# A recommendation net: the last part's second half worked off by feature groups, its layer 0 without transposes back, and the logits as 16 rows

## The reference, cut to what matters

```python
x = dense_inputs                                   # 2048 x 13
for W, b, g, be in bot:                            # 13 -> 512 -> 256 -> 64
    x = _bn(relu(x @ W + b), g, be)                # batch norm over all 2048 rows
embs = vmap(lambda tbl, idx: tbl[idx])(emb_tables, sparse_inputs)   # 26 rows of 64 for each batch
T = concatenate([embs, x[:, None, :]], axis=1)     # 27 vectors of 64
Z = einsum('bnd,bmd->bnm', T, T)                   # all pairs
R = concatenate([x, Z[:, iu, ju]], axis=1)         # 64 + 351 columns
h = R
for W, b, g, be in top:                            # 415 -> 512 -> 256 -> 1
    h = _bn(relu(h @ W + b), g, be)
return sigmoid(h)
```

## Time and profile before

| what | value |
|---|---|
| median of three runs | 573.51 us (572.97 to 573.55) |
| profiled execution, its own time | 573.65 us |
| its span, first to last instruction | 571.8 us |
| TensorE busy, weight loads busy | 374.6 us (66%), 281.1 us (49%) |
| VectorE, ScalarE, GpSimd busy | 238.8 us (42%), 189.5 us (33%), 388.8 us (68%) |
| mean granted clock of TensorE | 0.763 of full speed |
| chain that ended last, by engine | POOL 55%, issue 19%, PE 18% |

### The profile page before, as it was taken

How to read it: one execution, slowest core, us unless ns; L and a number is a source line. 1 busy time by engine, 2 the same in 40 slices (tenths; PEclk the granted TensorE clock), 3 DMA queues, 4 the chain that set the end, 5 groups by cost and what they waited for, 6 DMA issues and landing times.

```text
span 571.8 us, 16640 instructions
## 1 busy us (share of the span) xinstructions
PE 374.6 (66%) x5806; PEld 281.1 (49%) x5827; DVE 238.8 (42%) x650; ACT 189.5 (33%) x509; POOL 388.8 (68%) x419
## 2 busy tenths in 40 slices
PE   5959768678687572755729181754738182777995
PEld 2328536566565462543517171553526172566682
DVE  5773354644445342424323242423324242455522
ACT  4752144434244141323214041322314041464223
POOL 5777777777777777777777777777777777770100
PEclk9999886896786877585857666585858567598999
DMA  8322122222212221222122121222212121220000
GB/s 240 62 29 28 28 27 31 30 26 31 30 29 30 27 31 29 31 27 30 27 28 30 28 31 26 30 27 29 31 29 29 26 30 26 30 28 7 2 0 2
DMA packets 17500, 18.49 MB, mean 32 GB/s; under 512 B 9302, under 2 KB 10589, under 8 KB 17278
## 3 DMA queue, kind: packets, MB, share of 16 engines
q0 software_dynamic: 13088, 13.43, 17.6%
q1 hardware_dynamic: 4330, 3.96, 2.3%
HBM read 17.35 MB, written 0.01 MB: 30 GB/s over the span
## 4 chain that ended last, share of the span: by engine, by line
POOL 55%; issue 19%; PE 18%; DVE 2%; ACT 2%; DMA 1%; SPq 0%; POOLq 0%; DVEq 0%; ACTq 0%
POOL emb L367 52%; PE l_bank L442 6%; PE l_bank L458 5%; POOL emb L380 3%; PE l_bank L448 3%; PE l_bank L472 2%; PE l_bank L564 1%; DMA emb<-table,stage 1%; ACT Zs L306 1%; PE z_bank L400 1%; DMA par<-params 1%; DVE TT L916 0%; PE l_bank L611 0%; PE l_bank L561 0%; PE tr_bank L536 0%
## 5 line engine op out<-in xcount | busy, mean ns | idle before, releaser
L367 POOL DMA_INDIRECT emb<-table,stage x385 | 363.9, 945 | 120.3 <-issue 117.1
L306 ACT ACTIVATE Zs<-z_bank 27x112 f32<-27x112 f32 (+3 forms) x272 | 92.1, 339 | 200.8 <-PE z_bank L507 179.5
L493 PE MATMUL tr_bank<-ident,emb 128*128 128x128 f32 x195 | 39.1, 330 | 125.8 <-DMA emb<-table,stage 105.5
L280 DVE COPY Zs<-z_bank 27x112 f32<-27x112 f32 (+3 forms) x272 | 88.6, 326 | 51.1 <-PE z_bank L507 43.6
L521 PE MATMUL l_bank<-Zs,tw_sb 128*128 128x128 f32 x840 | 107.2, 281 | 0.0
L521 PEld LDWEIGHTS l_bank<-Zs,tw_sb 128*128 128x128 f32 x840 | 103.1, 199 | 0.0
L916 DVE COPY TT<-tr_bank 128x512 f32<-128x512 f32 (+1 forms) x60 | 54.6, 975 | 97.3 <-PE tr_bank L493 96.8
L493 PEld LDWEIGHTS tr_bank<-ident,emb 128*128 128x128 f32 x195 | 25.9, 163 | 137.5 <-issue 104.0
L507 PE MATMUL z_bank<-TT 64*27 64x26 f32 x3840 | 63.5, 219 | 31.8 <-issue 18.4
L507 PEld LDWEIGHTS z_bank<-TT 64*27 64x27 f32 x3840 | 55.4, 134 | 42.1 <-issue 38.1
L927 DVE BATCH_NORM_STATS2 stats_t<-h_part 128x128 f32 x60 | 17.7, 294 | 112.7 <-ACT hidden_hi L705 110.1
(11 more groups left out here) (130 smaller groups left out, 279.2 us busy)
## 6 DMA issues: line engine op xcount, KB each, us to landing
emb<-table SPq DMA_DIRECT2D x640, 0.2 KB
emb<-table,stage POOLq DMA_INDIRECT x409, 2.8
emb_sp<-table SPq DMA_DIRECT2D x256, 0.2 KB
tw_sb<-tw0x SPq DMA_DIRECT2D x1, 1792.0 KB
bw_sb<-bw SPq DMA_DIRECT2D x1, 512.0 KB, 3.8
tw_sb<-tw SPq DMA_DIRECT2D x1, 512.0 KB
twx_sb<-twx SPq DMA_DIRECT2D x1, 256.0 KB
idx_raw<-idx SPq DMA_DIRECT2D x1, 169.0 KB, 2.5
```

What stands on the lines that cost most here:

```text
L280: last = copy(dst, src[:, :, ZC * q:ZC * q + w])
L306: return nc.scalar.activation(dst, src, ACT.Copy)
L367: pool.indirect_dma_start(out=emb[:, s, k, h, :], out_offset=None, in_=table, in_offset=bass.IndirectOffsetOnAxis(ap=stage[:, s, col:col + ...
L493: tr = nc.tensor.transpose(tr_bank[g % 2][:, c * P:(c + 1) * P], emb[:, s, k, :, :].rearrange("p h d -> p (h d)"), ident[:, :])
```

## The change

Five things change.

1. The second half of the last part gets groups of its own, pairs 0 to 6, 6 to 12 and 12 to 13 (the first keeps its three groups). x becomes feature 0 of TT, the embeddings 1 to 26, and a pair's tile column c and quadrant q are now the quotient and rest of the second feature by four; so columns c 0 to 2 of Zs need only the first group, 3 to 5 the second, 6 the third. Z, its copies and layer 0 follow group by group.
2. In that half a Z matmul takes a block of batches: two in the first two groups, four in the third. The half has its own tile TT_last with 32 columns for a batch, so the stationary operand is 64 or 128 columns, and the moving one the group's features of all batches of the block (2 x 12, 2 x 12, 4 x 2). Only the blocks of a batch with itself are copied (take_last: eight copies per engine of 13x48, eight of 25x48, four of 27x16). The first half's Z goes to one bank and is copied in 8 copies per engine; all copies from Z now read every fourth column.
3. Layer 0 of the last part has the weights stationary, as in the loop, 128 batches at once, column by column c, each for all four blocks, started when its c is there. pre0, last_back and the four transposes back are gone. Relu is four ScalarE operations of 128x128; the high parts of the last part are made behind w1_hi, and layer 1 waits for last_lo only before its fourth chunk. The number of idle matmuls in the last part changes from 7, 2, 1, 5, 15 to 7, 2, 10, 8, 1, 7, 11.
4. The logits are written as 16 rows of 128 batches: for each of the two k 16 matmuls of 32 columns over 128 batches, whose weight has one column that isn't zero, in place of 4 over 512. ScalarE's three operations are 128x128, mean_of picks the 16 rows by a column of par, and 16 rows of 512 bytes are stored in place of 4 of 2 KB.
5. At the start VectorE computes the row numbers for SyncE before it clears Zs, and clears TT_last and tw2_col too.

```diff
-LAST_GROUPS = ((0, 8), (8, 12), (12, 13))
+Z_BATCHES = (2, 2, 4)
+LAST_GROUPS = (((0, 8), (8, 12), (12, 13)), ((0, 6), (6, 12), (12, 13)))
...
+        def take_last(copy, g, quadrants):
+            c0, c1 = group_tiles(*LAST_GROUPS[1][g])
+            m0, m1 = NQ * c0, min(NQ * c1, NF)
+            rows = m1 + 1
+            for j in quadrants:
+                z = Z_BATCHES[g]
+                src = last_z_bank[1][g][QUAD * j:QUAD * j + rows, 0:RX * z * (m1 - m0)].rearrange(
+                    "p (x b m) -> p x b m", b=z, m=m1 - m0)[:, :, j % z, :]
+                for q in range(NQ):
+                    m = quadrant_columns(q, c0, c1)
+                    if not len(m):
+                        continue
+                    dst = Zs[QUAD * q:QUAD * q + rows, c0:c0 + len(m), :].rearrange(
+                        "p c (h x j) -> p h x j c", h=2, j=NQ)[:, 1, :, j, :]
+                    last = copy(dst, src[:, :, m[0] - m0:m[-1] + 1 - m0:NQ])
+            return last
...
-                if net == "top":
-                    pe.wait_ge(last_lo, K0)
                 for ch in range(CHUNKS):
+                    if net == "top" and ch == CHUNKS - 1:
+                        pe.wait_ge(last_lo, K0)
...
+            def last_z_group(g):
+                first = len(LAST_GROUPS[0])
+                pe.wait_ge(last_tt_v, first + g + 1)
+                if g < len(LAST_GROUPS[1]) - 1:
+                    pe.wait_ge(last_tt_a, first - 1 + g + 1)
+                c0, c1 = group_tiles(*LAST_GROUPS[1][g])
+                m0, m1 = NQ * c0, min(NQ * c1, NF)
+                z = Z_BATCHES[g]
+                w = z * (m1 - m0)
+                for x in range(RX):
+                    for j in range(0, NQ, z):
+                        some = last_T(1)[:, x * NQ + j:x * NQ + j + z, :]
+                        mm = nc.tensor.matmul(last_z_bank[1][g][QUAD * j:QUAD * (j + z), x * w:(x + 1) * w],
+                                              some.rearrange("p b n -> p (b n)"), some[:, :, m0 + 1:m1 + 1],
+                                              start=True, stop=True)
+                mm.then_inc(last_z_done, 1)
+
+            def last_layer0(c, blocks=range(K0)):
+                part = slice(LAST * 2 * UNIT, B)
+                for o in blocks:
+                    cols = slice(o * P, (o + 1) * P)
+                    if c < 0:
+                        mm = nc.tensor.matmul(l0_bank[o][:, 0:2 * UNIT], twx_sb[:, cols], x_all[:, part],
+                                              start=True, stop=False)
+                    else:
+                        mm = nc.tensor.matmul(l0_bank[o][:, 0:2 * UNIT], tw0_sb[:, c, cols], Zs[:, c, :],
+                                              start=False, stop=(c == ZC - 1))
+                    if c == ZC - 1:
+                        mm.then_inc(last_l0, 1)
...
             keep_clock(7, z_bank[0])
+            last_z_first()
+            pe.wait_ge(l0_relu, LAST * K0)
+            last_layer0(-1)
+            keep_clock(2, tr_bank[1])
             last_transposes(1, 0)
+            keep_clock(10, tr_bank[1])
+            last_z_group(0)
+            keep_clock(8, tr_bank[1])
+            last_taken(1)
+            last_taken(2)
+            last_layer0(0)
+            last_layer0(1)
             last_transposes(1, 1)
+            last_layer0(2)
+            keep_clock(1, tr_bank[0])
+            last_z_group(1)
             last_transposes(1, 2)
+            keep_clock(7, tr_bank[1])
+            last_taken(3)
+            last_layer0(3)
+            last_z_group(2)
+            last_layer0(4)
+            last_layer0(5)
+            last_taken(4)
+            last_layer0(6, (0, 2, 1, 3))
+
+            keep_clock(11, z_bank[0])
             layer1("top")
...
-                for j in range(CHUNKS):
-                    mm = nc.tensor.matmul(out_bank[0][QUAD * j:QUAD * (j + 1), :], tw2_rep[:, k, :],
-                                          hidden1[:, k, j * CHUNK:(j + 1) * CHUNK],
-                                          start=(k == 0), stop=(k == K1 - 1))
+                for j in range(LB):
+                    for q in range(NQ):
+                        first = (q * LB + j) * P
+                        mm = nc.tensor.matmul(out_bank[0][QUAD * q:QUAD * (q + 1), 0:P],
+                                              tw2_col[:, k, j * QUAD:(j + 1) * QUAD], hidden1[:, k, first:first + P],
+                                              start=(k == 0 and j == 0), stop=(k == K1 - 1 and j == LB - 1))
```

More of the change, by code:

```diff
@@ L70 @@
 CHUNKS = B // CHUNK
-CU = CHUNK // UNIT
+LB = CHUNK // P
+LROW = QUAD // LB
 PW = NF
@@ L96, with quadrant_columns, group_tiles @@
 PARAMS["top", "W", 2] = (sum(w for _, w in PARAMS.values()), K1)
-NPARAM = sum(w for _, w in PARAMS.values())
+NPARAM = sum(w for _, w in PARAMS.values()) + 1
 def group_pairs(g):
     return range(g * GROUP, min((g + 1) * GROUP, TP))
-def quadrant_columns(q):
-    return min(ZC, NF - ZC * q)
+def quadrant_columns(q, c0=0, c1=ZC):
+    return range(q + NQ * c0, min(q + NQ * c1, NF), NQ)
+def group_tiles(k0, k1):
+    return k0 // 2, (k1 + 1) // 2
 def rec_program(nc, idx, sp_idx, table, dense_t, params, identity, bw0, bw1, bw2, tw0x, twx, tw1, out):
@@ L539, in last_transposes @@
                 tr.then_inc(last_transposed, 1)
-            def last_z(h):
-                pe.wait_ge(last_tt_v, (h + 1) * len(LAST_GROUPS))
-                pe.wait_ge(last_tt_a, upper_copies((h + 1) * len(LAST_GROUPS)))
-                pe.wait_ge(tt_x_written, PARTS)
-                for y in range(2):
-                    for x in range(y * RX // 2, (y + 1) * RX // 2):
-                        for j in range(NQ):
-                            one = TT[0:D, h, x * NQ + j, :]
-                            mm = nc.tensor.matmul(z_bank[y][QUAD * j:QUAD * j + V, x * ZM:(x + 1) * ZM],
-                                                  one, one[:, 1:V], start=True, stop=True)
-                    mm.then_inc(last_z_done, 1)
@@ L554, in last_layer0 @@
-            def last_layer0(h, t, columns):
-                for c in columns:
-                    for f in range(2):
-                        acc = l0_bank[t][f * UNIT:(f + 1) * UNIT, 0:P]
-                        cols = slice(f * HALF + t * P, f * HALF + (t + 1) * P)
-                        if c < 0:
-                            mm = nc.tensor.matmul(acc, x_all[:, last_columns(h)], twx_sb[:, cols],
-                                                  start=True, stop=False)
-                        else:
-                            mm = nc.tensor.matmul(acc, Zs[:, c, h * UNIT:(h + 1) * UNIT],
-                                                  tw0_sb[:, c, cols], start=False, stop=(c == ZC - 1))
-                return mm
@@ L586, in _, with last_z_first @@
-            for g in range(len(LAST_GROUPS)):
+            def last_z_first():
+                for x in range(RX):
+                    for j in range(NQ):
+                        one = last_T(0)[:, x * NQ + j, :]
+                        mm = nc.tensor.matmul(last_z_bank[0][QUAD * j:QUAD * j + V, x * ZM:(x + 1) * ZM],
+                                              one, one[:, 1:V], start=True, stop=True)
+                mm.then_inc(last_z_done, 1)
[8 more added lines that the diff above has]
+                w = z * (m1 - m0)
+                for x in range(RX):
+                    for j in range(0, NQ, z):
[3 more added lines that the diff above has]
+                                              start=True, stop=True)
+                mm.then_inc(last_z_done, 1)
@@ L1050 @@
     for row, (n, m) in enumerate(zip(*np.triu_indices(V, k=1))):
-        q, c = divmod(m - 1, ZC)
-        tw0x[QUAD * q + n, c] = w0[D + row]
+        first, second = (0, n) if m == NF else (n + 1, m)
+        c, q = divmod(second, NQ)
+        tw0x[QUAD * q + first, c] = w0[D + row]
     cols = idx.reshape(UNIT * 2, PARTS, TP, 2)
```

236 lines of the change are left out of this document (100 added, 136 removed).

## The result

The changed kernel takes 579.28 us (median of five runs, 576.47 to 579.91) against 573.54 us for the one before, run beside it on the same chip (five runs, 572.97 to 574.49): the ratio is 1.0074, 95% interval 1.0047 to 1.0101. By either the change is slower, the forecast of 574.2 was wrong, and the median lies above the range, whose upper end was 577.0. The profiled execution took 579.91 us, its span 578.0. Of experiment e13 one execution, the profiled one, ran 1,427 us, with TensorE's operations longer (layer 0 in the loop 954 ns a record for 278) while the granted clock read 1.00; its ratio leaves it out, its median doesn't.

A forecast was written before the change was run, and what follows sets the result against it. GpSimd's gathers were taken to bound the kernel until about 515 us, TensorE's chain after. Last part +1.65, relu stretch -0.15, logits -0.77 made +0.7 on 573.65: 574.4, runs' median 0.14 lower, 574.2 us; range 571.3 to 577.0.

The forecast's parts named there:

- rival (b): Third Z group: TensorE's clock falls, layer 0's twelve matmuls cost 2.7 us more, 577 us results; chance 0.10.
- Rows 5: Old profile's clock windows in the last part: lower in 512 to 515 us, upper 516 to 522, lower 526 to 529.
- the twelve matmuls: Layer 0 behind the third group: 2.7 us, and 0.2 of latency, ending at 533.8 us.
- (d): Rival on the last part's copies: reading every fourth column doubles an element's price, 3.0 us more, 577.2 us; chance 0.07.
- my sum: Last part +1.65, relu to layer 1 -0.15, logits -0.77: +0.7 us on 573.65, so 574.4 profiled; chance 0.53.
- the prices of the groups: Z of the second half: 2.0, 2.0 and 3.5 us for the three groups, 7.5 in all.
- (a): Rival on Z groups: block columns load at the Z row's rate, 1.53 us each, 4.6 for three, 571.3 us; chance 0.20.
- (c): Rival on Z groups: the two column halves load in turn, first two groups 3.5 us each, 577.2 us; chance 0.10.
- The strided copies: Second half's copies from Z: 2.06 us for eight of 48 elements, 0.8 for four of 27x16.
- Back-to-back issue gap: Skill's rule for small matmuls: some 25 ns start-to-start at least; groups would cost 1.6, 1.6, 0.8, sum 3.5 us less.
- The logits: End of the kernel: ScalarE 0.97 us less, TensorE 0.2 more, in all 0.77 less; bounds 0.4 and 1.0.
- The start: VectorE's two more clears and one multiplication, perhaps 2.5 us, covered by a wait for ScalarE: no effect on the time.

The follow-up runs named there:

- e13: Changed kernel, groups (2, 2, 4), with ten and nine idle matmuls for eight and seven in the gaps ahead of layer 0: 577.76 us, 1.0053 of the kernel before.
- e3: Changed kernel with two idle matmuls after each of the first three quarters of the third group: 581.04 us, 1.0099 of the kernel before.
- e5: Changed kernel once more, nothing altered: 577.92 us, 1.0074 of the kernel before.
- e15: The kernel of e13 once more, for its trace: 580.49 us, one execution.
- e16: The kernel of e13 once more again, for its trace: 577.84 us, one execution.
- e1: Changed kernel with blocks of one batch in all three Z groups of the second half: 577.06 us, 1.0029 of the kernel before.
- e2: Changed kernel with blocks of two in the third group as well (2, 2, 2): 575.88 us, 1.0010 of the kernel before.
- e7: Changed kernel with blocks of two in the third group, and ten and nine idle matmuls for eight and seven: 574.16 us, 0.9995 of the kernel before.
- e9: Changed kernel with the second half's Z in one piece, blocks of one, other numbers of idle matmuls: 573.60 us, 0.9983 of the kernel before.
- e12: The kernel before with only the change's start (VectorE's order, one clear more): 574.09 us, 1.0000 of the kernel before.
- e11: The two-group kernel e6 with ten idle matmuls in each gap: 572.63 us, 0.9969 of the kernel before.
- e6: Changed kernel with two Z groups (pairs 0 to 6, 6 to 13) instead of three, blocks of two: 571.87 us, 0.9961 of the kernel before.
- e10: The two-group kernel e6 with blocks of one batch: 573.27 us, 0.9982 of the kernel before.

## Why the prediction was wrong

**The step that failed** is the chance and the price of rival (b), that TensorE's clock falls in the third group. It had 0.10, because "dense work lies ahead of and behind each group now", and the sum went by a clock of 1.00 from 515 on. Dense work around the group was no safeguard: all five traces of kernels with the (2, 2, 4) form (the changed kernel, e3, e5, e15, e16) show the fall inside or just behind the third group, with TensorE without a gap from its start, and in e15 and e16 with the gaps ahead of it filled. e1 and e2, with blocks of one and two, had the fall behind the third group too; of the kernels with three groups only e7's trace has none there. Rows 5 showed a fall in 526 to 529, inside dense layer 0 work; I read it only as the end of the idle time ahead of it. In one-microsecond stretches of that trace the clock is 1.00 through the idle time, 0.84 in 525 to 526, where layer 0 begins (525.58), and 0.50 from there to 529. The price was too small as well: I counted the twelve matmuls (2.7; measured 2.6 in the profiled execution), and not the group itself, which with the fall inside it took 5.65 instead of 3.66. And the range was drawn too narrow by the prediction's own terms: the middles of (b) to (d) are 577.0 to 577.2, so an upper end of 577.0 leaves out at least half of them, and not a third.

**The account of the 5.6 us** by which layer 1 came late (at 542.45, forecast 536.85): the first half's Z began 0.5 late (509.16, in the trace before 508.66); from there to the third group it took 19.03 instead of 18.74 (527.4 less 508.66), 0.3; the group took 5.65 to the next row's start instead of 3.5, of which 0.2 is its price at the upper clock (3.66 in e5) and 2.0 the clock; layer 0 5.49 instead of 2.9, of which 2.94 is e7's value at the upper clock, so 2.55 the clock; 0.1 lies behind it. The clock accounts for 4.5 in this execution, and for 1.6 in e5 and e16, where it fell later. 579.91 - 4.5 is 575.4, a microsecond above the 574.4 of my sum; e5 and e16, less 1.6, give 576.4 and 576.2. So even at the upper clock the change would have been no gain; no run showed the (2, 2, 4) form with the clock held, so these figures are worked out and not measured.

**Right in size:** the prices of the groups, forecast 2.0, 2.0 and 3.5, measured 2.05, 2.05 and 3.7 at the upper clock, and that of two tiles whatever moves (4, 24 or 28 columns: 2.03, 2.05, 2.05); so rivals (a) at 1.53 and (c) at 3.5 are out. With four tiles the weight columns don't show as a price: 128 records took 1.28 us with 32 columns (e9) and 1.29 with 27 (before). The strided copies, forecast 2.06 and 0.8, measured 2.08 and 0.80: (d) is out. By the rule of the Trainium skill, "TensorE: Matmul & The Clock Gate", Back-to-back issue gap, which I weighed, the groups would have cost 1.6, 1.6 and 0.8; the traces give 32 ns a record in two tiles and 115 in one, over that floor, so it isn't the price there, and 10 in four (e1's 110 records in 1.10 us), under it, so it doesn't hold there. The logits: forecast 0.77 less, measured 0.87 less, inside the bounds; of the 0.2 for 48 more records nothing shows (1.08 us a round, before 1.07). The start: nothing (e12).

**Right in place, and the reason why the change could not gain:** TensorE waits for no gather after 512, as forecast, so cutting the work finer hides nothing any more, and a further group adds its Z to one chain. From the start of the second group to layer 1 it is 13.50 us with three groups of blocks of two (e7) and 11.47 with two (e11), both at the upper clock: 2.03 us, the third group's Z. Two groups (e6) win 2.1 us on the kernel before, 0.87 of it by the logits; three in blocks of two (e7) are even with it.

**What stays open.** What in the third group's form pulls the clock down isn't known: it differs from the group of blocks of two in the number of matmuls, in the width of the weights and in the length. That three groups in blocks of two can hold the clock rests on e7's one trace, which had a fall ahead of the first group, against e2's, which had none there and fell behind the third; so neither the form nor the filling is shown as the cause. One group of Z was tried only with blocks of one and the stall. And the last gathers began between 514.36 and 515.84 over the kernels, whose gathers are the same, so some tenths of each difference are not the change's.

## What to carry to other kernels

Cut work into pieces only as long as a piece still waits for its data; when the last wait for a transfer is gone, each further piece only lengthens the chain. Here two groups beat three. Price small matmuls with new weights by the weight columns and the number of tiles side by side and not by the moving columns, and look at the granted clock of the very stretch in which many of them run, since a busy share of 1.00 says nothing of it. Where a forecast depends on the clock, price its fall over all the work that would run under it, and give it the chance that the old trace's own falls suggest.

## What the runs showed of the hardware that was not expected

TensorE stopped for 2.1 to 2.4 us on "issue" in e1, e9 and e10, after 109 to 128 records of one-batch matmuls at some 10 ns each, while the only transfers of the stretch were two packets of 0.03 MB together on the instruction queue; with blocks of two, half the instructions in more time, there was no such stall. But e2, without a stall, had the same two packets, and the first groups of e1 and e10, 128 such records in 1.4 us, had no stall behind them. That TensorE ran ahead of the supply of its instructions is a guess; no run took it apart.

The lower clock came in stretches in which TensorE was busy the whole time (3.00 of 3.00 us, 100%). Six idle matmuls strewn into the third group (e3) did not stop the fall.
